# Pair masks on ScalarE, attention terms laid out in reading order, projections one step sooner

## What is computed

```python
x = x + _L0_conv_ref(_gn(x), L0_conv_w_in, L0_conv_w_qk, L0_conv_w_out, L0_conv_rel_bias)   # attention one
x = x + _L1_conv_ref(_gn(x), L1_conv_w_qkv, L1_conv_w_out)                                 # attention two

# attention two, B, F, N, D = x.shape, 16 heads of 16, chunks of 4 * 16 = 64 tokens
qkv = (x.reshape(B, T, D) @ w_qkv.T).reshape(B, T, 3, H, HD)
k_cat = jnp.concatenate([k_prev, k], axis=2)      # keys of the chunk before and of this one
v_cat = jnp.concatenate([v_prev, v], axis=2)
scores = jnp.einsum('bclhd,bcmhd->bchlm', q, k_cat) * scale
scores = jnp.where(valid[None, :, None, None, :], scores, jnp.finfo(scores.dtype).min)
attn = jax.nn.softmax(scores, axis=-1)
out = jnp.einsum('bchlm,bcmhd->bclhd', attn, v_cat).reshape(B, T, H * HD) @ w_out.T
```

## Time and profile before

| | us |
|---|---|
| median of 3 runs | 183.56 (182.95 to 183.91) |
| the profiled execution | 182.27 |
| its span, first to last instruction | 180.5 |
| mean granted TensorE clock | 0.981 |

### The profile page before, as it was taken

One profiled execution on the slowest core, in us unless ns is written; L12 is line 12 of the kernel. 1 busy time (PEld: TensorE's weight loads), 2 busy tenths in 40 slices (PEclk: granted clock), 3 DMA queues, 4 the chain that ended last, 5 costly groups with the idle time before them and its releaser, 6 DMA issues.

```text
span 180.5 us, 4317 instructions
## 1 busy us (share of the span) xinstructions
PE 153.7 (85%) x1582; PEld 132.1 (73%) x1582; DVE 110.9 (61%) x326; ACT 91.0 (50%) x186; POOL 110.8 (61%) x170
## 2 busy tenths in 40 slices
PE   7989879779798898999399884998989978979963
PEld 7577768667795798778397674997879867868751
DVE  1636487935582963386154994459878478797130
ACT  1339219857775478467333355234574443445520
POOL 0310535779842357347999969985699879990000
PEclk9999999999999999999879999699999999999999
DMA  6419700000000000369202792038802694010101
GB/s 178 131 36 307 242 0 5 0 0 5 2 0 0 4 2 0 120 194 216 59 0 116 199 218 51 0 153 244 193 3 116 210 215 107 29 33 0 62 10 54
DMA packets 9589, 15.85 MB, mean 88 GB/s; under 512 B 952, under 2 KB 5432, under 8 KB 9568
## 3 DMA queue, kind: packets, MB, share of 16 engines
q1 hardware_dynamic: 9008, 15.22, 30.6%
q10 hardware_dynamic: 560, 0.35, 0.8%
HBM read 10.31 MB, written 5.26 MB: 86 GB/s over the span
## 4 chain that ended last, share of the span: by engine, by line
PE 48%; DMA 17%; DVE 14%; POOL 7%; ACT 6%; issue 5%; SPq 1%; DVEq 0%; POOLq 0%; ACTq 0%
DMA K<-k_terms 8%; PE bank L586 6%; PE bank L566 6%; POOL QP L370 5%; PE bank L598 4%; DMA Q<-q_terms 4%; PE bank L677 3%; DMA k_terms<-KHL 3%; PE bank L608 3%; PE bank L493 3%; PE bank L687 3%; PE bank L617 3%; DVE NM L970 3%; PE bank L746 2%; PE bank L724 2%
## 5 line engine op out<-in xcount | busy, mean ns | idle before, releaser
L370 POOL TENSOR_SCALAR QP<-Q,con 96x256 fp32r<-96x256 f32 x64 | 57.9, 919 | 2.5 <-DMA Q<-q_terms 2.1
L1192 ACT ACTIVATE PT<-bank 128x512 f32<-128x512 f32 x64 | 38.3, 600 | 33.4 <-PE bank L617 17.5
L358 POOL TENSOR_SCALAR SB<-SB,NM 128x256 f32<-128x256 f32 x64 | 30.0, 483 | 14.4 <-DVE NM L966 14.0
L966 DVE CUSTOM_DVE_ANT_0 SB<-bank,Tk 128x256 f32<-128x256 f32 x64 | 24.5, 420 | 20.9 <-PE bank L586 20.5
L970 DVE TENSOR_REDUCE NM<-bank 128x4 f32<-128x512 f32 x32 | 21.9, 685 | 23.4 <-PE bank L598 23.2
L598 PE MATMUL bank<-K,QP 96*128 96x128 f32 x128 | 21.4, 291 | 6.9 <-DMA K<-k_terms 6.7
L598 PEld LDWEIGHTS bank<-K,QP 96*128 96x128 f32 x128 | 17.6, 199 | 9.8 <-DMA K<-k_terms 7.6
L977 DVE TENSOR_TENSOR SB<-bank,NM 128x512 f32<-128x512 f32 x32 | 22.1, 692 | 1.1
L586 PE MATMUL bank<-KH,QM 128*128 128x256 f32 x64 | 20.7, 344 | 0.7 <-ACT QM L1185 0.7
L617 PE MATMUL bank<-con,SB 128*128 128x128 f32 x128 | 20.2, 283 | 0.0
L608 PE MATMUL bank<-con,SB 128*128 128x128 f32 x128 | 19.7, 277 | 0.0
(11 more groups left out here) (142 smaller groups left out, 271.2 us busy)
## 6 DMA issues: line engine op xcount, KB each, us to landing
Q<-q_terms SPq DMA_DIRECT2D x12, 256.0 KB, 5.8
K<-k_terms SPq DMA_DIRECT2D x12, 256.0 KB, 6.3
q_terms<-WQK SPq DMA_DIRECT2D x4, 512.0 KB, 2.7
k_terms<-KHL SPq DMA_DIRECT2D x4, 512.0 KB, 2.9
Tk<-bias_rows SPq DMA_DIRECT2D x4, 384.0 KB, 5.0
X<-x SPq DMA_DIRECT2D x4, 256.0 KB, 4.2
y<-Y SPq DMA_DIRECT2D x8, 128.0 KB, 1.7
VB<-w_qkv SPq DMA_DIRECT2D x1, 768.0 KB, 7.9
```

Of the source, the lines that this page charges most:

```text
L358: last = nc.gpsimd.tensor_scalar(rows_of, rows_of, -1.0, NM[:, i % 2, 2 * u + nt:2 * u + nt + 1], ALU.mult, ALU.add)
L370: last = nc.gpsimd.tensor_scalar(QP[0:ROWS, idx % QRING, :, v, :], Q3[0:ROWS, b % 2, :, g, c * CHUNK:(c + 1) * CHUNK], con[0:ROWS, C_SIDE ...
L966: last = V.tensor_tensor_reduce(SB[:, idx % SRING, nt * CH:(nt + 1) * CH], half, Tk[:, u, nt * P:nt * P + CH], 1.0, LOWEST, ALU.add, ALU.m ...
L1192: A.activation(PT[:, u, :], bank[Z_BANK + u % 2][:], ACT.Exp, scale=-SCALE if is_a(i) else SCALE).then_inc(p_ready, 1)
```

## The change

- `pair_queries` goes from GpSimd to ScalarE. One call now serves a chunk (two blocks): two activations over 96 partitions x 1024 elements (copy, with the mask column as scale), in even steps, right behind the exponent of that step. `QP` is a ring of two chunks; the semaphore `qp_ready` counts chunks, and TensorE waits for it in even blocks alone.
- `q_terms` and `k_terms` have the layout (part, 32 channels, pair group, tokens). Each is written with four transfers of 32 partitions, 2 KB rows, and read with two: one onto 64 partitions (Q: 0 to 63, K: 32 to 95) and one onto 32 (Q: 64 to 95, K: 0 to 31), 8 KB a partition.
- The preparation of units 4 to 7 starts one step sooner (`XT_B` to `V_B`). So do unit 3's projections behind the first, and the output steps of units 0 to 3.
- `window_values` has one wait less on GpSimd.

```diff
-        QRING = 4
-        QP = sb("QP", [P, QRING, PAIRS, 2, CHUNK], F32R)
+        QRING = 2
+        QP = sb("QP", [P, QRING, PAIRS, 2, 2, CHUNK], F32R)
...
-        q_terms = nc.dram_tensor("q_terms", (BATCH, P, 2, 2 * TOK), F32, kind="Internal").ap()
-        k_terms = nc.dram_tensor("k_terms", (BATCH, P, 2, 2 * TOK), F32, kind="Internal").ap()
+        q_terms = nc.dram_tensor("q_terms", (BATCH, 2, GRP, PAIRS, 2 * TOK), F32, kind="Internal").ap()
+        k_terms = nc.dram_tensor("k_terms", (BATCH, 2, GRP, PAIRS, 2 * TOK), F32, kind="Internal").ap()
...
-        TIMES_A = [(range(1, 2), (-6, -4, -3, -2)), (range(2, 3), (-5, -3, -3, -2)), (range(3, BATCH), (-9, -7, -7, -6))]
-        XT_B, GM_B, GV_B, Q_B, K_B, V_B = -13, -12, -11, -8, -7, -6
-
-
-        FINISH = [(IN_A, (9, 12), (14, 14), (15, 15), (17, 17)),
+        TIMES_A = [(range(1, 2), (-6, -4, -3, -2)), (range(2, 3), (-5, -3, -3, -2)), (range(3, BATCH), (-9, -8, -8, -7))]
+        XT_B, GM_B, GV_B, Q_B, K_B, V_B = -14, -13, -12, -9, -8, -7
+
+
+        FINISH = [(IN_A, (9, 12), (13, 13), (14, 14), (16, 16)),
...
+            def put_terms(b, terms, hl, ready, written):
+
+                sp.wait_ge(ready, BATCH + b + 1)
+                for a in range(PAIRS):
+                    sp.dma_start(terms[b, :, :, a, :].rearrange("s p n -> p s n"), hl[a * GRP:(a + 1) * GRP].bitcast(F32)).then_inc(written, 16)
+
+            def get_terms(b, terms, dst, both, high, written, loaded):
+
+                sp.wait_ge(written, 16 * PAIRS * (b + 1))
+                sp.dma_start(dst[GRP * both:GRP * (both + 2)], terms[b].rearrange("s p a n -> (s p) (a n)")).then_inc(loaded, 16)
+                sp.dma_start(dst[GRP * high:GRP * (high + 1)], terms[b, 0].rearrange("p a n -> p (a n)")).then_inc(loaded, 16)
+
             def terms(b):
 
                 n, i = b % 2, BATCH + b
-                sp.wait_ge(q_ready, i + 1)
-                sp.dma_start(q_terms[b], QHL[:].bitcast(F32)).then_inc(q_written, 16)
-                sp.wait_ge(k_ready, i + 1)
-                sp.dma_start(k_terms[b], KHL[:].bitcast(F32)).then_inc(k_written, 16)
+                put_terms(b, q_terms, QHL, q_ready, q_written)
+                put_terms(b, k_terms, KHL, k_ready, k_written)
                 if b >= 2:
-                    sp.wait_ge(qk_ready, BLK * (b - 1))
-                sp.wait_ge(q_written, 16 * (b + 1))
-                for s, part in enumerate((0, 1, 0)):
-                    sp.dma_start(Q3[GRP * s:GRP * (s + 1), n].rearrange("p a g n -> p a (g n)"),
-                                 q_terms[b, :, part, :].rearrange("(a p) n -> p a n", p=GRP)).then_inc(q_loaded, 16)
+                    sp.wait_ge(qp_ready, NCH * (b - 1))
+                get_terms(b, q_terms, Q3[:, n].rearrange("p a g n -> p (a g n)"), 0, 2, q_written, q_loaded)
                 if b >= 2:
                     sp.wait_ge(s_done, BLK * (i - 1))
-                sp.wait_ge(k_written, 16 * (b + 1))
-                for s, part in enumerate((0, 0, 1)):
-                    sp.dma_start(K3[GRP * s:GRP * (s + 1), n].rearrange("p a g n -> p a (g n)").bitcast(F32),
-                                 k_terms[b, :, part, :].rearrange("(a p) n -> p a n", p=GRP)).then_inc(k_loaded, 16)
+                get_terms(b, k_terms, K3[:, n].rearrange("p a g n -> p (a g n)").bitcast(F32), 1, 0, k_written, k_loaded)
...
-            def pair_queries(i, u):
...
+                if not is_a(i) and u % 2 == 0:
+                    pe.wait_ge(qp_ready, (i - BATCH) * NCH + u // 2 + 1)
...
+            def pair_queries(i, c):
+
+                b = i - BATCH
+                if c == 0:
+                    act.wait_ge(q_loaded, 32 * (b + 1))
+                if b * NCH + c >= QRING:
+                    act.wait_ge(s_done, i * BLK + 2 * (c - QRING) + 2)
+                for v in range(2):
+                    last = A.activation(QP[0:ROWS, c % QRING, :, :, v, :].rearrange("p a g n -> p (a g) n"),
+                                        Q3[0:ROWS, b % 2, :, :, c * CHUNK:(c + 1) * CHUNK].rearrange("p a g n -> p (a g) n"), ACT.Copy,
+                                        scale=con[0:ROWS, C_SIDE + v:C_SIDE + v + 1])
+                last.then_inc(qp_ready, 1)
...
                 ahead = t + AHEAD
                 if ahead < BATCH * BLK:
                     head_queries(ahead // BLK, ahead % BLK)
+                elif ahead < UNITS * BLK and ahead % 2 == 0:
+                    pair_queries(ahead // BLK, ahead % BLK // 2)
```

More of the change, by code:

```diff
@@ L214, in build @@
         s_done, max_ready, sub_ready, subb_ready = (sem(n) for n in ("s_done", "max_ready", "sub_ready", "subb_ready"))
-        qk_ready = sem("qk_ready")
+        qp_ready = sem("qp_ready")
         qm_ready = sem("qm_ready")
@@ L359, in below_max @@
                 last.then_inc(sub_ready, 1)
-            def pair_queries(i, u):
-                b, idx = i - BATCH, (i - BATCH) * BLK + u
-                c, g = u // 2, u % 2
-                if u == 0:
-                    pool.wait_ge(q_loaded, 16 * TERMS * (b + 1))
-                if idx >= QRING:
-                    pool.wait_ge(s_done, i * BLK + u - QRING + 1)
-                for v in range(2):
-                    last = nc.gpsimd.tensor_scalar(QP[0:ROWS, idx % QRING, :, v, :], Q3[0:ROWS, b % 2, :, g, c * CHUNK:(c + 1) * CHUNK],
-                                                   con[0:ROWS, C_SIDE + v:C_SIDE + v + 1], None, ALU.mult)
-                last.then_inc(qk_ready, 1)
             def low_x(b):
@@ L385, in scale_b, with window_values @@
                 nc.gpsimd.tensor_tensor(grs[:], gve[:], mhalf[:], op=ALU.pow).then_inc(grs_ready, 1)
-            def window_values(b, ahead, masked):
+            def window_values(b, ahead):
                 n = b % 3
@@ L422, in _ @@
                 for i in due(t, V_B + 2, IN_B):
-                    window_values(i - BATCH, ahead, masked)
+                    window_values(i - BATCH, ahead)
         @block.tensor
@@ L598, in scores_b @@
                     last = nc.tensor.matmul(bank[S_BANK + u % 2][:, a * P:(a + 1) * P],
-                                            QP[0:ROWS, idx % QRING, a].rearrange("p v n -> p (v n)"), window, start=True, stop=True)
+                                            QP[0:ROWS, c % QRING, a, g].rearrange("p v n -> p (v n)"), window, start=True, stop=True)
                 return last
@@ L631, in scores @@
                 elif u == 0:
-                    pe.wait_ge(k_loaded, 16 * TERMS * (i - BATCH + 1))
-                if not is_a(i):
-                    pe.wait_ge(qk_ready, idx - BATCH * BLK + 1)
+                    pe.wait_ge(k_loaded, 32 * (i - BATCH + 1))
+                if not is_a(i) and u % 2 == 0:
+                    pe.wait_ge(qp_ready, (i - BATCH) * NCH + u // 2 + 1)
                 if idx >= BATCH * BLK + 2:
@@ L1146, in projected @@
                         if b:
-                            act.wait_ge(q_written, 16 * b)
+                            act.wait_ge(q_written, 16 * PAIRS * b)
                         A.activation(QHL[:, 0, :], f[:], ACT.Copy).then_inc(qh_ready, 1)
@@ L1151, in projected @@
                         if b:
-                            act.wait_ge(k_written, 16 * b)
+                            act.wait_ge(k_written, 16 * PAIRS * b)
                         A.activation(KHL[:, 0, :], f[:], ACT.Copy).then_inc(kh_ready, 1)
```

6 lines of the change are left out of this document (1 added, 5 removed).

## The result

| | before | changed |
|---|---|---|
| median of the runs beside one another, us | 183.28 (182.95 to 183.91) | 174.61 (173.17 to 175.02) |
| the profiled execution | 182.27 | 175.02 |
| its span | 180.5 | 173.1 |
| mean granted clock, from 24 us of the span on (nothing is recorded before that) | 0.981 | 0.993 |

The ratio is 0.9592, with a 95% interval of 0.9531 to 0.9653; the two medians alone give 0.953. By the medians the kernel is faster by 8.7 us, by the ratio by 7.5, where I forecast 4.0: right direction, and the gain about double.

The account below looks back on a forecast made before the run. TensorE's idle time, mainly 6.7 us of K-load waits plus half-clock stretches, was taken as the bound. 87.0 + 20.3 + 20.6 + 18.4 + 12.1 + 18.1 = 176.5 us span; against the median, 179.6 us, range 173.0 to 184.5.

Parts of the forecast that it names:

- start of unit 4: TensorE's first scores of unit 4 at 87.0 us instead of 88.54, with 1.44 us of projection moved ahead of them.
- unit 7 to step 62: From unit 7's first scores to its last needing a new mask pair: 12.1 us against 11.14, light steps held at 4.0.
- the end: The stretch behind unit 7's step 62: 18.1 us against 17.96, since ScalarE comes to it 0.1 later.
- 2.2 us for a pair: Two mask activations on ScalarE over 96 x 1024, 1157 ns each less overlap; low end 2.0, high end 3.7 us each.
- the loop: Scores, exponent, mask pair, then TensorE's scores two steps on: two steps cannot take under 4.0 us.
- ScalarE leaves none of 18 of 19 us: ScalarE with the masks is busy 18.0 us in units of some 19 to 20, so its idle time cannot hide them.
- rival A: The masks on ScalarE hide; stalls (6.7 us) and half-clock stretches (3.4) go, nothing is given back: 173.5 us; chance 0.23.
- Edit 1: New terms layout, four writes and two loads: write to K's landing 11.1 us against 11.4, worth nothing to count on alone.
- Edit 2: Projections one step sooner: unit 4's K terms ready at about 74.8 instead of 77.06, its 3.06 us stall gone.
- Edit 3: Masks moved from GpSimd to ScalarE: 64 GpSimd instructions of 919 ns go, ScalarE gains 8.8 us per unit.
- Rival B: Idle in light pairs of units 4, 5 and 7 drops the clock, 1.7 us each; four times, 186.4 us; chance 0.13.
- Rival C: K's load is no sooner, landing at 88 for unit 4, while the masks' price stays: 182.4 to 183.5 us; chance 0.12.

## Why the prediction was right or wrong

| step of the sum | forecast | changed kernel | the other profile of it |
|---|---|---|---|
| start of unit 4 | 87.0 | 88.47 | 86.70 |
| unit 4 | 20.3 | 19.06 | 20.79 (half clock) |
| unit 5 | 20.6 | 19.20 | 19.19 |
| unit 6 | 18.4 | 16.65 | 16.64 |
| unit 7 to step 62 | 12.1 | 11.80 | 11.80 |
| the end | 18.1 | 17.88 | 18.0 |
| span | 176.5 | 173.06 | 173.1 |

**The step that failed** is the size of the activation, 1024 elements for 512, and with it "2.2 us for a pair": it took 1.32. The rate per element, the loop and its order held (1142 ns for 1157, 3.86 us for 4.0). The experiment with the assumed size gives the price of this one step, 4.1 us. That it also lands near the forecast, 179.01 for 179.6, is in part luck: its units 5 and 6 are each 0.9 us shorter than in the sum and unit 7 is 0.55 longer, and as a ratio it is 0.9883, where the forecast is 0.978.

With 1.36 us for a pair (2 x 0.713 less the overlap of some 0.07), the same stepping gives 18.6, 18.9, 16.3, 11.8 and 17.95 us by my estimate, so 87.0 + 83.55 = 170.6 of span. It thus prices the factor of two at 5.9 us, 1.8 more than the runs do. Against that stand 1.5 us at the start of unit 4, and 1.1 us over units 4 to 6. In that stretch lie the waits for `VB` (1.23 us) and for the low part (0.44 before unit 5), which the stepping didn't hold; that they are the whole of it wasn't shown.

A third of the miss of 5.0 us is none of this. I had added 1.3 us, since the profiled execution of the kernel before lay that far below its median; that of the changed kernel lay 0.4 above (175.02 against 174.61). That makes 1.7 us, and the span itself was missed by 3.4. (The rest is 2.0 us around the span for 1.8.)

"ScalarE leaves none of 18 of 19 us" fell with the size: it is busy for 13.6 of 19.06 us in unit 4 and 14.7 of 19.20 in unit 5. The argument against rival A rested on that number; with the right size A is the likeliest case, and its 173.5 is 1.1 us under what was measured.

**Start of unit 4.** The wait of 3.06 us is gone, as said, and K is no longer late. But 88.54 - 3.06 = 85.48, the end of TensorE's work for attention one, and then come: 0.24 us at the start of the pipeline (step 5's scores begin at 27.75, in the trace before at 27.51), 0.64 in attention one, 1.53 of the next image's projection (I said 1.44), and 0.58 for the low part of its input. Sum 88.47. The 0.64 is the shift of the steps of unit 3 and of the outputs, costed at nothing with ends of -0.5 and +0.5: from step 5's scores to the end of attention one's work it is 57.97 us before and 58.61 after (to 86.36). The marks are these rows, first of the kernel before, then of the changed one:

```profile
83.92 0.36 PE L586 MATMUL bank<-KH,QM 128*128 128x256 f32 x1
...
85.04 0.44 PE L714 MATMUL bank<-con,ON 128*128 128x128 f32 x2
```

```profile
85.02 0.44 PE L700 MATMUL bank<-con,ON 128*128 128x128 f32 x2
85.21 0.36 PE L572 MATMUL bank<-KH,QM 128*128 128x256 f32 x1
...
85.76 0.60 PE L594 MATMUL bank<-con,SB 128*128 128x128 f32 x4
```

To the scores of step 31 (83.92 and 85.21) it is 1.05 us more, 56.4 before and 57.5 after, but these transposes now stand ahead of them. The three experiments with the old steps take 56.4 as well, and those with the new ones 57.5, with or without the masks on ScalarE, so it belongs to the steps. With the value copy first it is 57.2, with the low part in halves 56.9 and with both 56.7: so some 0.8 us of it go away with the order of the value copy and the halves. The 0.58 is a wait I hadn't thought of: the projection that now stands ahead of unit 4 needs GpSimd's low part of that image's input:

```profile
87.89 0.74 PE L552 MATMUL bank<-XTl,WTh 128*128 128x256 f32 x4 [0.58 <-POOL XTl L370]
```

**Edit 1.** SyncE's queue in the changed kernel, unit 5:

```profile
94.26 1.72 SPq L290 DMA_DIRECT2D k_terms<-KHL  x4
...
98.10 0.51 SPq L295 DMA_DIRECT2D K<-k_terms  x1
98.66 0.58 SPq L296 DMA_DIRECT2D K<-k_terms  x1
```

From the write's issue to the loads' release it is 3.84 us; I said 3.9. In the kernel with layout and masks TensorE still waits for K, so that its trace has the landing as well, here for unit 5:

```profile
97.45 1.72 SPq L290 DMA_DIRECT2D k_terms<-KHL  x4
```

```profile
108.25 0.67 PE L584 MATMUL bank<-K,QP 96*128 96x128 f32 x4 [1.90 <-DMA K<-k_terms]
```

10.8 us (97.45 to 108.25), and 10.5 in unit 4 (76.03 to 86.50), against 11.4 before and 11.1 forecast. So the path is 0.6 to 0.9 us shorter than before and the forecast was 0.3 to 0.6 too long. "The loads at 220 GB/s still" was wrong in part. Half-microsecond windows of the changed kernel, last column GB/s, over unit 5's Q load and K load:

```profile
100.50:101.00 0.50, 0.50 (x12) 0.31 (x15) 0.47 (x2) 0.50 (x2) 0.00 (x0) 1.00 1.05 229
...
102.50:103.00 0.50, 0.50 (x8) 0.50 (x5) 0.47 (x2) 0.45 (x1) 0.00 (x0) 1.00 1.36 442
```

The Q load, onto partitions 0 to 63 and 64 to 95, stays at 180 to 262, but the K load reaches 442 (426 in unit 4's). Both have rows of 8 KB and the same sizes, and differ in the partitions: K's larger piece lies on 32 to 95. In the trace before, no half microsecond of unit 5's loads is above 287. This is what the prediction had kept as its low end (1.5 us for that piece, not 2.4). The rule of the Trainium skill that was cited, SBUF — State Buffer, "Door 1: The DMA port swizzle" (64 partitions from 0 no faster than 32), agrees with the Q load's 180 to 262 GB/s; for 32 to 95 the sum had taken it over without a row, and that piece was faster. Five other profiles with the new layout have such a half microsecond in unit 5's loads too (426 to 492), and three others with the old one have none above 287. No run changes the partitions alone.

The edit is worth nothing that can be told by itself (0.9965 [0.9914, 1.0016]), though TensorE waits for K there. In the changed kernel no one waits for K.

**Edit 2.** It does what the forecast says: the stalls are gone, and the half-clock stretches behind them. Terms of unit 4 are written from 75.78, and not 74.8.

**Edit 3.** On its own it costs 1.3%; how much of that is the longer half clock isn't known. Beside edit 2 its price at 1024 elements is 4.1 us more than at 512, and at 512 it can't be told from that of no masks at all (0.45 us) or of masks on GpSimd (0.9671 against 0.9653, in two jobs).

**Rival B** (the clock falls) came in part: 1.7 us, as sized, but once and not three or four times, in two of three profiles of the changed kernel. By the prediction's own sign ("if half-clock stretches remain") this counts against it. The place isn't the light pairs either, it is behind 1.24 us of idle in unit 4; behind the 0.66 us in unit 7's light pair the clock stays at 1.00. And 0.71 us was not the longest harmless idle stretch of the trace before: TensorE waited 1.09 us for VectorE at 145.97, at a clock of 1.00. **Rival C** (K no sooner) is excluded: no wait. The statement that "TensorE waits for QP 0.5 to 1.5 us in even steps" holds in one place (0.66 us). The upper end of the range, 184.5, is further than half of the way to B, which is 183.0.

## What to carry to other kernels

Read the size of an operation that moves from the row of the operation that it replaces (96x256 for one block, so 512 for two) and check the new shape against it: one factor of two is worth 4.1 us here, as much as the whole gain forecast. A step shift has a price of its own, in the stage that it moves through (0.64 us) and for inputs that are no longer early (0.58). Before an engine in a loop is given more work, work out the loop's time with it and compare it with what the other engines need anyway: here 1.3 us a pair cost next to nothing, and 0.9 us more a pair cost 4.1. And check how far the one profiled execution lies from the median before its distance goes into a forecast: from one kernel to the other it moved by 1.7 us.
